# Unread bfloat16 products on TensorE ahead of the waits of the gradient-memory layer

## The reference, cut to what matters

```python
def _mem_loss(p, k_t, v_t):
    W1 = p[:D * D].reshape(D, D)
    W2 = p[D * D:].reshape(D, D)
    pred = jax.nn.silu(k_t @ W1.T) @ W2.T
    return jnp.sum((pred - v_t) ** 2)
...
for c0 in range(0, S, CHUNK):                       # S = 256, CHUNK = 64
    g = _grad_fn(W_state, k[:, sl], v[:, sl]) * GRAD_SCALE
    g = g * jnp.minimum(MAX_GRAD_NORM / gn, 1.0)    # gn: norm of g, one per token
    (S_state, W_state), Wtraj = jax.lax.scan(step, (S_state, W_state), xs)
    h = jax.nn.silu(jnp.einsum('btd,btod->bto', q[:, sl], W1t))
    outs.append(jnp.einsum('bto,btpo->btp', h, W2t))
retrieved = jnp.concatenate(outs, axis=1)
out = retrieved @ Wo.T                              # then a norm and a gate
```

## Time and profile before

| what | value |
|---|---|
| median of 3 runs | 4809.53 us |
| lowest and highest of them | 4800.02 and 4809.84 us |
| the profiled execution | 4812.54 us, of which the span is 4810.8 us |
| TensorE busy | 3834.0 us (80% of the span) |
| VectorE busy | 3405.1 us (71%) |
| ScalarE busy | 2397.4 us (50%) |
| clock granted to TensorE, mean over the span | 0.87 |

### The profile page before, as it was taken

How to read it: one execution, slowest core, us unless ns; L and a number is a source line. 1 busy time by engine, 2 the same in 40 slices (tenths; PEclk the granted TensorE clock), 3 DMA queues, 4 the chain that set the end, 5 groups by cost and what they waited for, 6 DMA issues and landing times. The chain is left out here.

```text
span 4810.8 us, 75801 instructions
## 1 busy us (share of the span) xinstructions
PE 3834.0 (80%) x28914; PEld 2206.9 (46%) x28979; DVE 3405.1 (71%) x5269; ACT 2397.4 (50%) x3237; POOL 1425.0 (30%) x1078
## 2 busy tenths in 40 slices
PE   4740988999999999999984838849985858888883
PEld 3630445666666666666652514424433422222231
DVE  6469675878777877878774246667754658888868
ACT  2120224666666666666652125526652437767772
POOL 0000432666666666666663250000000000000000
PEclk5565998999999999999995659969986869999996
DMA  0010840000000000000002164145520433323300
GB/s 20 1 55 0 191 117 28 1 15 15 1 15 1 15 1 15 1 15 1 1 1 97 39 158 56 30 77 84 85 36 22 94 77 51 50 42 53 50 2 9
DMA packets 155463, 194.79 MB, mean 40 GB/s; under 512 B 23685, under 2 KB 117502, under 8 KB 154468
## 3 DMA queue, kind: packets, MB, share of 16 engines
q1 hardware_dynamic: 144068, 167.17, 17.3%
q0 software_dynamic: 9856, 22.67, 1.8%
q10 hardware_dynamic: 1184, 0.12, 0.0%
HBM read 145.03 MB, written 42.42 MB: 39 GB/s over the span
## 5 line engine op out<-in xcount | busy, mean ns | idle before, releaser
L3121 POOL TENSOR_TENSOR arena<-arena 128x512 f32<-128x512 f32 (+1 forms) x768 | 1133.2, 1477 | 629.9 <-ACT arena L3075 575.7
L2568 ACT ACTIVATE arena<-ps 128x1024 f32<-128x1024 f32 (+1 forms) x688 | 703.2, 1023 | 332.5 <-PE ps L2493 321.9
L2586 DVE TENSOR_REDUCE arena<-ps 128x2 f32<-128x826 f32 (+1 forms) x576 | 564.8, 981 | 182.2 <-PE ps L2439 173.9
L3137 DVE TENSOR_TENSOR arena<-arena 128x1024 f32<-128x1024 f32 (+1 forms) x448 | 653.2, 1497 | 34.9 <-ACT arena L3104 34.9
L3159 DVE TENSOR_TENSOR arena<-ps,arena 128x512 f32<-128x512 f32 (+1 forms) x768 | 530.3, 691 | 108.8 <-ACT arena L3069 75.3
L2439 PE MATMUL ps<-arena 48*128 48x413 bf16 (+3 forms) x1920 | 437.0, 334 | 133.8 <-DVE arena L2586 66.8
L3069 ACT ACTIVATE arena<-ps 128x1024 f32<-128x1024 f32 (+1 forms) x448 | 410.5, 960 | 200.6 <-PE ps L2997 194.8
L3075 ACT ACTIVATE arena<-arena 128x1024 f32<-128x1024 f32 (+1 forms) x448 | 425.0, 992 | 60.4 <-DVE arena L3137 57.9
L2512 PE MATMUL ps<-arena 128*9 128x256 f32 (+2 forms) x5504 | 437.1, 390 | 10.3 <-ACT arena L2556 7.5
L2997 PE MATMUL ps<-arena 64*128 64x256 f32 (+1 forms) x3328 | 427.4, 391 | 5.9 <-ACT arena L3091 1.3
L3011 PE MATMUL ps<-arena 128*64 128x256 f32 (+1 forms) x3328 | 411.1, 387 | 6.4 <-ACT arena L3075 6.4
(11 more groups left out here) (661 smaller groups left out, 5357.4 us busy)
## 6 DMA issues: line engine op xcount, KB each, us to landing
arena<-ctx_parts SPq DMA_DIRECT2D x96, 200.1 KB
arena<-ctx_parts SPq DMA_DIRECT2D x192, 100.1 KB
arena<-fs_rows SPq DMA_DIRECT2D x128, 128.0 KB, 6.7
arena<-in_ctx_feat SPq DMA_DIRECT2D x8, 1601.0 KB, 6.4
arena<-in_ctx SPq DMA_DIRECT2D x16, 768.0 KB
arena<-diff_att_stack SPq DMA_DIRECT2D x60, 192.0 KB, 6.6
ctx_parts<-arena SPq DMA_DIRECT2D x24, 400.2 KB, 7.4
arena<-in_ctx_feat SPq DMA_DIRECT2D x8, 800.5 KB, 9.3
```

The costliest lines, as they stand in the source:

```text
L2568: act.activation(self.prob[0:rows, u % 3, :], self.ps[0:rows, 2 * (u % 2):2 * (u % 2) + 2, :].rearrange("p n c -> p (n c)"), ACT.Exp).then ...
L2586: ins = dve.tensor_reduce(dst[:, :, j // 2], self.ps[:, 4:6, 0:hi - lo], AX.X, ALU.max)
L3121: pool.tensor_tensor(acc[0:rows, u % 2, :], before, sc[0:rows, u % 2, t, :], ALU.add).then_inc(added, 1)
L3137: dve.tensor_tensor(e, e, mb[0:rows, u % 2, None, :].to_broadcast([rows, n, 2 * S]), ALU.subtract).then_inc(sub_done, 1)
```

## The change

A new function `keep_busy` issues products whose results nobody reads: the stationary operand is the first 128 columns of the identity, seen as bfloat16 (128 rows), the moving operand is all 256 columns of it, and the result goes to a PSUM bank that holds nothing needed at that time. `memory_chunk` calls it 40 times ahead of the first step of chunk 0, 2 to 4 times ahead of each of the waits inside a chunk, and 30 times behind its last step. That is 57 products per chunk (55 in the last, which has no update), and 40 more in chunk 0: 266 in all. Nothing else is changed.

```diff
+def keep_busy(env, pe, bank, count):
+
+    filler = env.ident[:, :].bitcast(BF16)
+    for _ in range(count):
+        pe.matmul(env.ps[:, bank, 0:2 * P], filler[:, 0:P], filler, start=True, stop=True)
...
         def _(pe):
+            if c == 0:
+                keep_busy(env, pe, 7, 40)
             for b in range(B):
                 ins = pe.matmul(bank(0)[:, b, :], m["Wst"][:, 0, b, :], kT[:, b, :], start=True, stop=True)
             ins.then_inc(z_ready, 1)
...
             ins.then_inc(p_ready, 1)
+            keep_busy(env, pe, 7, 4)
             pe.wait_ge(h0_ready, 1)
...
             ins.then_inc(pred_ready, 1)
+            keep_busy(env, pe, 7, 4)
             pe.wait_ge(dp_ready, 1)
...
             ins.then_inc(dh_ready, 1)
+            keep_busy(env, pe, 7, 4)
             pe.wait_ge(da_ready, 1)
...
+            keep_busy(env, pe, 7, 4)
             pe.wait_ge(cg_ready, 1)
...
             if not last:
+                keep_busy(env, pe, 7, 2)
                 pe.wait_ge(cgw_ready, 1)
...
+            keep_busy(env, pe, 7, 4)
             pe.wait_ge(h_ready, 1)
...
             ins.then_inc(g2_ready, 1)
+            keep_busy(env, pe, 5, 2)
             pe.wait_ge(hab_ready, 1)
...
+            keep_busy(env, pe, 5, 3)
             pe.wait_ge(gm2_ready, 1)
             for b in range(B):
                 ins = pe.matmul(bank(0)[:, b, :], cg[:, 0, b, :], GM2[:, b, :], start=False, stop=(b == B - 1))
             ins.then_inc(out_ready, 1)
+            keep_busy(env, pe, 5, 30)
```

## The result

The changed kernel is slower: 4828.3 us (median of 20 runs) against 4802.15 us for the kernel before (20 runs). The ratio is 1.0051, with a 95% interval of 1.0034 to 1.0067, which is 16 to 32 us and in the middle 24.5 us.

A forecast was written before the change was run, and what follows sets the result against it. TensorE and VectorE hand results on in a chain, TensorE at the low clock; chunks 8.5 + 3.6 + 5.2 less 4.0 in the output gave +13.3 us, 4823 us for the median, range 4808 to 4833.

The forecast's parts named there:

- The price of one product: One `keep_busy` product on TensorE: 0.209 us at the low clock, 0.110 us at the high one.
- The fall: In each chunk, the clock's grant drops back to 0.50 about 2 us behind each dense run.
- the sum: All terms from chunk 0 to the output function: 8.5 + 3.6 + 5.2 - 4.0 = +13.3 us.
- a chunk's sets: The products ahead of waits inside a chunk: 3.11 us at the low clock, 1.85 in the last chunk.
- The output function's return: `memory_output`, begun behind a dense run, runs partly at the high clock: -4.0 us, between -2.0 and -6.3.
- The first rival: The clock stays up through all four chunks: about -23 us, 4787 us; chance 0.11.
- The second: In each chunk the clock lasts longer, through L566: +7.2 us in all, 4817 us; chance 0.20.
- The third: The clock never rises in the chunks or the output: +28 us, 4837 us; chance 0.04.

The follow-up runs named there:

- the run with many more: Denser products inside the chunks, 45 behind each and 20 behind the last, against the changed kernel; ratio 1.0078 to the kernel before.
- the first four experiments: Changed kernel cut to only the 40, only the 27 inside, only the 30 behind chunks 0 to 2; whole with 32 rows: 1.0028, 1.0049, 1.0004, 1.0077.

## Why the prediction came out as it did

The mechanism held: products that no wait hides are paid in full, the dense runs raised the clock, and it fell again ahead of the steps in the middle of each chunk. The price of one product held. At the low clock forty took 8.69 us in the run with 32 rows, (8.69 - 0.418)/39 = 0.212 us each against 0.209. At the high clock 21 took 2.47 us in the run with many more, (2.47 - 0.273)/20 = 0.110 as forecast. And the 40 took 6.94 us against 6.7. In the trace of after the clock rose 4.1 to 5.1 us after the first product of each dense run, where I took 4.8. By the rule of "TensorE: Matmul & The Clock Gate" (Trainium skill, section "Why this matters for your kernels") the filled chunk should have stayed at the high clock; the trace disagrees, with 29.91 of 30.60 us busy at a grant of 0.50.

The fall was less regular than I took it to be. I had it 2 us behind each dense run. It came 2.4 us behind at two of the five places, and 4.9 to 5.6 us behind at the other three, where the clock lasted until just ahead of L560 (98.4 us, and the step began at 98.92). The early fall in chunk 1 costs some 0.6 us: 37.95 us against 37.4 in chunk 2.

Two terms of the sum were mis-sized, and together they make up its 6.1 us.
- Inside the chunks I priced a set at 0.209 us for each product. The step behind it then begins 0.12 us later than that, and the sets ahead of L560 and L566 aren't quite hidden, so a chunk's sets cost 4.15 us at the low clock and not 3.11 (the run with only the inside sets). That is the larger part of what chunks 0 to 3 cost above the forecast: 9.5 + 5.2 + 5.5 = 20.2 against 17.3, or 2.9 us.
- The output function's return, for which I took -4.0 between -2.0 and -6.3, was -0.8 in the trace of after and -4.0 with the last 30 alone: 3.2 us. I had taken the clock to fall 2 us or more into the first set, L696. In the trace of after it fell 1.4 us into it, which saved 7.16 - 5.88 = 1.3 us there. And I had left out that L699 lost something: before, the clock rose 1.4 us ahead of its end, and after only 0.8, so it took 6.61 us in place of 6.09.

With both the stretch is +19.4 and not +13.3. The first rival fell (the clock does not hold at the change's density). The second had the longer clock right at three places, but it gave nothing more: L560 still took 1.91 us and L566 1.48. The third fell too (the clock did rise).

That the median of 4828.3 us lies so near the forecast of 4823 is partly luck. The forecast started from 4809.53 us, the median of three runs; over 20 runs the kernel before had 4802.15. From there the forecast's 13.3 would have given 4815, and from 4809.53 the measured 24.5 would have given 4834.

What stays open is the distance between the stretch and the timing. The timed differences of the first four experiments, 13.4, 23.5, 1.9 and 36.9 us, all lie 4 to 9 us above their stretches' 5.9, 14.1, -3.4 and 32.7, and with 24.5 against 19.4 the whole change does so too. Each timed difference is uncertain by about 8 us to either side; only the stretch of the 27 inside lies outside its interval (15 to 32 us). The four share the same runs of the kernel before (median 4797.7 us), and a common error of these would explain most of it, but the whole change was timed against others. The two versions that were timed later, against 18 runs with a median of 4812.1 us, show no such distance: 37.5 against 38.6 with many more products (the interval is 21 to 54), and -5.8 against -7.2 with the dense runs behind other work. So the whole times that I expected for the four (5 to 6, 11 to 13, -3 to -0.5 and 28 to 32 us) were all too low. The cause wasn't tested.

## What to carry to other kernels

Work that only keeps an engine busy is free just where the engine waits for something longer than it. Here that was behind each chunk and under the scans of the input function; ahead of a step on the critical path (the chain of steps that sets the time) each product is paid in full, with a gap for each set besides. Before filling waits to hold a clock, look in the same trace for the nearest stretch that did hold it, and compare how dense its products were and how many rows they had. If the fill needs as much time as the faster steps give back, look for one long dense step with a wait ahead of it, and raise the clock in that wait: in the input function this took 4.3 us off in the trace.

## What the runs showed of the hardware that was not expected

- An unbroken run of forty bfloat16 products of 32 rows (8.6 us) left the grant at 0.50; the same run with 128 rows raised it after 5 us.
- The float32 stream of 64 rows in the input function was granted 0.50 while it was busy for 13.83 of 13.90 us. With dense runs of 128 rows ahead of its steps they took 3.62 and 3.64 us in place of 7.06 and 7.03, at a grant of 1.00. Whether the stream itself keeps the clock up isn't separated: in the traces of before and after the clock fell only 2.1 to 5.6 us behind a dense run.
- Products with only 32 stationary columns but 128 rows were granted 1.00 from 21.5 to 27.9 us in that run. Before, with nothing in their place, the clock fell 2.2 us behind the products ahead of them. Whether they can also raise it wasn't tried.
